# Graph layer on one core: the low halves of the scaled features move from DVE (one operation) to POOL (two operations)

## What is computed

```python
def _L0_gnn_ref(x, edge_index, W1, b1, W2, b2):
    ...
    deg = segment_sum(ones, dst); dinv = where(deg > 0, rsqrt(deg), 0.0)
    norm = dinv[src] * dinv[dst]
    ...
    h = x @ W;  msg = h[src] * norm[:, None];  agg = segment_sum(msg, dst)
    ...
xn = _layernorm(x, axis=-1)
x = x + _L0_gnn_ref(xn, ...) + _L0_mix_ref(xn[None], ...)[0]
x = x + _L0_ffn_ref(_layernorm(x, axis=-1)[None], ...)[0]
```

## Time and profile before

| | us |
|---|---|
| median of 2 runs (2003.83 and 2005.24) | 2004.53 |
| the profiled execution, its own time | 2000.85 |
| its span | 1999.0 |
| PE busy (94% of the span) | 1879.2 |
| DVE busy (59%) | 1182.2 |
| ACT busy (43%) | 851.9 |
| POOL busy (15%) | 299.6 |

### The profile page before, as it was taken

The page is one execution under the profiler, slowest core; times in us unless marked ns, Lnnn a source line. Parts: engine busy times, 40 slices in busy tenths (PEclk is TensorE's granted clock), DMA queues, the critical chain, the costliest instruction groups (busy, mean ns, idle before and its releaser), DMA issues. The chain is left out here.

```text
span 1999.0 us, 45233 instructions
## 1 busy us (share of the span) xinstructions
PE 1879.2 (94%) x18843; PEld 1409.5 (71%) x18843; DVE 1182.2 (59%) x2699; ACT 851.9 (43%) x1970; POOL 299.6 (15%) x417
## 2 busy tenths in 40 slices
PE   3599989999999999999979999999999999999598
PEld 3255555555555555555569999999999999998477
DVE  6899987666666666666515555555555555555322
ACT  1577765566566656666512222222222222222100
POOL 3143110000000000000020111111111111111033
PEclk7699989999999999999989999999999999999799
DMA  3133322323222232222344444444444444442087
GB/s 98 56 114 108 96 82 98 130 98 126 102 106 122 98 130 98 117 111 98 130 160 140 145 146 146 146 145 146 145 146 145 142 143 144 145 138 81 13 273 242
DMA packets 92701, 252.13 MB, mean 126 GB/s; under 512 B 14142, under 2 KB 59346, under 8 KB 79938
## 3 DMA queue, kind: packets, MB, share of 16 engines
q1 hardware_dynamic: 69225, 218.83, 30.8%
q10 hardware_dynamic: 21096, 25.65, 3.6%
q0 software_dynamic: 2176, 4.75, 0.9%
HBM read 131.99 MB, written 118.02 MB: 125 GB/s over the span
## 5 line engine op out<-in xcount | busy, mean ns | idle before, releaser
L1390 PE MATMUL ps<-hs,at 128*128 128x512 f16 x2401 | 667.1, 378 | 0.4 <-POOL at L1207 0.3
L1609 PE MATMUL ps<-at,big 128*128 128x128 f16 x9604 | 577.3, 219 | 6.5 <-DMA at<-at_scratch 6.5
L1609 PEld LDWEIGHTS ps<-at,big 128*128 128x128 f16 x9604 | 556.3, 98 | 34.3 <-issue 8.1
L1446 ACT CAST at<-ps 128x392 f16<-128x392 f32 x784 | 375.7, 487 | 286.7 <-PE ps L1351 271.3
L1351 PE MATMUL ps<-big 128*128 128x98 f16 x3136 | 470.8, 208 | 7.3 <-DVE big L1291 7.1
L1351 PEld LDWEIGHTS ps<-big 128*128 128x128 f16 x3136 | 297.0, 97 | 141.0 <-DVE big L1291 8.9
L1390 PEld LDWEIGHTS ps<-hs,at 128*128 128x128 f16 x2401 | 229.6, 97 | 148.2 <-issue 0.5
L1291 DVE TENSOR_TENSOR big<-iota_lo,key_lo 128x1024 f16<-128x1024 f16 x392 | 268.7, 685 | 0.0
L1291 DVE TENSOR_TENSOR big<-iota_hi,key_hi 128x784 f16<-128x784 f16 x392 | 219.3, 559 | 0.0
L1723 DVE SCALAR_TENSOR_TENSOR big<-ps,small,blogb 128x512 f32<-128x512 f32 x49 | 36.8, 751 | 230.6 <-PE ps L1645 230.6
L1826 POOL TENSOR_TENSOR key_lo<-key_lo,big 128x512 f32<-128x512 f32 (+1 forms) x49 | 61.9, 1264 | 706.6 <-ACT big L1784 706.6
(11 more groups left out here) (280 smaller groups left out, 2285.3 us busy)
## 6 DMA issues: line engine op xcount, KB each, us to landing
at_scratch<-at SPq DMA_DIRECT2D x49, 1568.0 KB, 5.2
at<-at_scratch SPq DMA_DIRECT2D x49, 1568.0 KB, 6.9
xT_scratch<-big SPq DMA_DIRECT2D x98, 128.0 KB, 1.8
big<-xT_scratch SPq DMA_DIRECT2D x49, 256.0 KB, 3.2
wT_scratch<-big ACTq DMA_DIRECT2D x49, 256.0 KB, 2.0
hs<-wT_scratch SPq DMA_DIRECT2D x49, 256.0 KB, 3.5
big<-in_x_dram SPq DMA_DIRECT2D x96, 128.0 KB, 2.3
x_scratch<-big ACTq DMA_DIRECT2D x48, 128.0 KB, 1.7
```

The lines of the kernel that those rows point to most:

```text
L1390: mm = te.matmul(ps[:, 2 + b, :], lhsT=at[:, b, k * P:(k + 1) * P], rhs=hs[:, k, :], start=(k == 0), stop=(k == T - 1))
L1446: a.copy(to.rearrange("p k (i j) -> p k i j", j=WIN), ps[:, BANKS[m % len(BANKS)], 0:UW * KC].rearrange("p (i k j) -> p k i j", i=UW, j=WI ...
L1609: mm = te.matmul(ps[:, b, c * NT:(c + 1) * NT], lhsT=hs2[:, k, h * C + c * P:h * C + (c + 1) * P], rhs=at[:, b, k * P:(k + 1) * P], start= ...
```

## The change

`halves` goes from DVE's stream. POOL gets `low_halves(t)`, between the gather and the addition of tile t: a product `xn * dsc` into a new buffer `scaled` (float32, 128 x 256), and the difference of `scaled` and the high half, written to `hs` as float16. Both count a semaphore `lows_made`, which also takes the place of `k4_zeroed`. `scaled` is one buffer, so the product of a tile waits for the difference of the tile before. `norm` gets a wait: the ring place of `xn` is written again only when the low half of the tile four before is done (`lows_made` counts the clearing of `k4_sum`, then two for each tile).

```diff
+            scaled = take([P, C])
...
                     if reached(t, RING):
                         dve.wait_ge(kx_done, t - RING + 1)
+                        dve.wait_ge(lows_made, 2 * (t - RING) + 3)
...
-                def halves(t, b):
-                    dve.wait_ge(hi_ready, t + 1)
-                    v.scalar_tensor_tensor(out=hs[0:rows(t), bass.ds(t, 1), C:2 * C].rearrange("p o c -> p (o c)"),
-                                           in0=xn[0:rows(t), b, 0:C], scalar=dsc[0:rows(t), bass.ds(t, 1)],
-                                           in1=hs[0:rows(t), bass.ds(t, 1), 0:C].rearrange("p o c -> p (o c)"),
-                                           op0=ALU.mult, op1=ALU.subtract)
...
-                    if reached(t, -1) and within(t, T - 1):
-                        halves(t + 1, (b + 1) % RING)
...
+                def low_halves(t, b):
+                    pool.wait_ge(hi_ready, t + 1)
+                    pool.wait_ge(lows_made, 2 * t + 1)
+                    g.tensor_scalar(scaled[0:rows(t), :], xn[0:rows(t), b, 0:C], dsc[0:rows(t), bass.ds(t, 1)], None,
+                                    ALU.mult).then_inc(lows_made, 1)
+                    pool.wait_ge(lows_made, 2 * t + 2)
+                    g.tensor_tensor(hs[0:rows(t), bass.ds(t, 1), C:2 * C].rearrange("p o c -> p (o c)"), scaled[0:rows(t), :],
+                                    hs[0:rows(t), bass.ds(t, 1), 0:C].rearrange("p o c -> p (o c)"),
+                                    ALU.subtract).then_inc(lows_made, 1)
...
                         gather_sources(t // WPS, t % WPS)
+                    low_halves(t, b)
                     pool.wait_ge(k4_ready, 2 * t + 2)
```

More of the change, by code:

```diff
@@ L623, in gps_layer @@
             k4_ready, k2n_ready, kx_done = sem("k4_ready"), sem("k2n_ready"), sem("kx_done")
-            k4_zeroed, k4_added = sem("k4_zeroed"), sem("k4_added")
+            lows_made, k4_added = sem("lows_made"), sem("k4_added")
             q2f_ready, q2_turned, q2T_stored = sem("q2f_ready"), sem("q2_turned"), sem("q2T_stored")
@@ L824, in _ @@
                 g = nc.gpsimd
-                g.memset(k4_sum, 0.0).then_inc(k4_zeroed, 1)
-                pool.wait_ge(k4_zeroed, 1)
+                g.memset(k4_sum, 0.0).then_inc(lows_made, 1)
+                pool.wait_ge(lows_made, 1)
                 def gather_sources(g, j):
```

## The result

The changed kernel takes 2019.24 us (median of 2 runs, 2018.86 and 2019.63) against 2004.53: ratio 1.0077, 95% interval 1.0057 to 1.0096. It is slower by 14.7 us; the forecast was 2006.0, the range ended at 2014. The profiled execution took 2019.63, its span is 2017.6.

What follows compares the result with a forecast made beforehand. PE was taken as the bound, except in seven key tiles, where it waits for DVE's normalised rows. L707 removed -2.7, holds +3.3, addition at L699 +0.9 sum to +1.5 on 2004.53: 2006.0 us, range 2000 to 2014.

Steps and rivals of the forecast that it cites:

- The step that failed: PE loses 2.08 us in each of seven key tiles (those with DVE's burst), nothing elsewhere but in first and last tiles.
- L707 removed, -2.7: Removing DVE's low halves shortens the path to L699 by 0.39 us in seven key tiles; nothing in 42 other tiles.
- Durations on POOL: POOL's new operations: product taken as 0.50 us, between 0.28 and 0.73; difference 0.67 us.
- Holds in the burst, +0.47 a key tile: Product and difference hold DVE's burst for 0.30 to 0.67 us a key tile; 0.47 taken, seven times +3.3 us.
- The walk through the tile: Key tile on the earlier timelines: product keeps L678 out +0.07 us, difference keeps L682 out +0.23.
- The addition at L699, +0.13: POOL's later addition holds L699 0 to 0.27 us more in key tiles; 0.13 taken, seven times +0.9 us.
- The gather: On POOL ahead of the product: 0.93 us in POOL's tile, with no hold on DVE in the sum.
- The new wait: norm's wait for the low half of four tiles earlier costs nothing while POOL keeps up.
- PE outside the key tiles: PE stays busy without a gap there, one tile taking 3.54 and 3.73 us.
- fall clear of the burst: Rival: product and difference meet DVE operations that POOL doesn't stretch; -2.7 us, or -4.2 with L699 missed; chance 0.20.
- set the pace of the stage: Rival: POOL becomes the bound, past a product of 0.65 us in early tiles; 2013.7 at product 1.0; chance 0.12.
- lengthen PE's ordinary tiles: Rival: DVE is held in every tile, 42 other tiles costing up to 0.42 us each, up to 2022; chance 0.10.

Runs made afterwards that it cites:

- e2: Changed kernel with four extra unused PE products one tile ahead of PE's wait in each of the seven key tiles: 2009.05 us, ratio 1.0019.
- e7: Kernel before, with the burst's last operation made twice, the first time into a spare tile, nothing new on POOL: 2018.98 us, ratio 1.0077.
- e10: Kernel before with the low halves made by nobody, zeros set once by POOL ahead of the first tile: 2009.72 us, ratio 1.0032.
- e6: Changed kernel with POOL's product also waiting for k2n of its tile: 2010.92 us, ratio 1.0037.
- e4: Changed kernel with xn in a ring of eight in place of four: 2017.55 us, ratio 1.0054.
- e5: Both makers: DVE's low halves as before, POOL's product and difference into a spare tile: 2031.44 us, ratio 1.0143.
- e11: Changed kernel with the burst's five operations laid over four tiles: 2003.68 us, ratio 0.9996.
- e3: Changed kernel with POOL's product waiting, in the seven key tiles, for the xn behind the burst: 2006.67 us, ratio 1.0004.

## Why the prediction was wrong, point by point

*The step that failed* is the one that turns DVE's lateness into time. It stands at the start, where a key tile loses 2.08 us "and nothing elsewhere but in its first and last tiles", and the sum takes it over: each hold counts at its own length, seven times, so a longer wait of PE costs its own length and no more. The sum had no term for the clock behind the wait, though the earlier trace rows has the clock as a column, at 1.00, and no step of mine asked whether it would stay there. e2 puts it back at 1.00 and takes 12.1 us out of the stage; e7 brings it down without the change. At the full clock the kernel would have come out at some +4 in the stage, by the growth of PE's waits. In e2, which also pays for its four products, it is +6.0, and e2's median, 2009.05 beside 2005.75, is inside the range.

*L707 removed, -2.7.* The right path and the wrong size: 1.6 by e10, because the burst moves onto the end of the gather, and where there is no gather L699 is held longer.

*Durations on POOL.* The difference was right (0.67 taken, 0.70 as a mean). The product was taken as 0.50, near the one-input row; with nothing in its way it takes 0.95 (at 132.35 us), above the bound of 0.73. The Trainium skill (GPSIMD Engine Reference, section 4.1, Engine selection) has one-input work at roughly line rate; measured, it was slower here than the addition with two inputs. The guess from L296, another operation at another size, was no bound.

*Holds in the burst, +0.47 a key tile.* Measured 0.19 + 0.07 + 0.35 = 0.61 in five key tiles, 0.65 in the last two, inside 0.30 to 0.67. The walk through the tile had the 0.07 of the third operation right and put 0.23 on the fifth; it had nothing on the first. *The addition at L699, +0.13:* 0.62 before and 0.62 after. *The gather* was priced at nothing, since L721 beside it was as short as ever in the kernel before. It costs 0.42 once POOL's next operation stands ready behind it (e6). So four of the seven key tiles came out at +0.64 at the full clock, not at +0.21; the first grew more, the last two less.

*The new wait* costs nothing, as said (e4). *PE outside the key tiles:* ahead of the first burst, and behind two of the key tiles, 3.54 and 3.73 as said; behind the other five not.

*The rivals.* POOL did not fall clear of the burst. It did not set the pace of the stage either, though the sign that I set for that, a product over 0.7, came. The sum put 0.14 between any two POOL instructions, which makes 2.89 + 0.95 = 3.84 of a tile ahead of the burst; measured it is 3.57, with gaps of 0.04 and 0.08 around the product. But this rival was nearer than the 0.12 says: 3.57 is over PE's 3.54, and in e5 and e11 POOL has next to no idle time. DVE's holds did not lengthen PE's ordinary tiles, 3.54 and 3.73 at the full clock; how much of DVE's 0.57 at the first burst comes from holds ahead of it is not shown. The rule of the Trainium skill (SBUF — State Buffer, section Who interferes with whom), that the other one is shut out for the whole instruction, gave about 2011. DVE's holds in the burst stayed inside my shorter bounds; POOL's product, though, was kept out for 1.95 - 0.95 = 1.0 us in the key tile shown.

*What stays open:* which waits bring the clock down. In the changed kernel one of 2.13 us did (at 140.74 us), one of 2.14 did not (180.28), one of 1.77 did (215.31); in e6 one of 1.62 did not; in e3 one of 1.51 with one of 0.58 close behind did, in the kernel before none of the seven of 1.21 to 1.51. The length of the wait alone doesn't tell it. Also open is why a gather holds L716 in the changed kernel and L673 in e10, and neither L721 before nor L716 in e6: e6 shows what undoes it for L716, not how it comes about.

## What to carry to other kernels

When PE is the engine that the kernel lives on, price a longer wait of PE twice: by its length, and by a tile at half the clock that may follow it; look at the granted clock in windows behind each wait, and ask how much longer than today's the wait would be. An operation that is moved to POOL takes a price with it if DVE's operations lie beside it, and it can make DVE pay for a neighbour on POOL that cost nothing before, here the gather. Undo and redo one half at a time: here the addition alone cost 28 us and the removal alone gave 1.6 (in the profiled stage), and neither says what the two give together.

## What the runs showed of the hardware that was not expected

- TensorE's clock fell to 1.2 GHz in the middle of a stage, behind many of the waits of 1.77 to 3.5 us, and behind some shorter ones with another close behind (e3: 1.11 and 0.77, 1.51 and 0.58); the tile behind then took up to 6.75 us (e4) in place of 3.73.
- A gather on POOL made a 128 x 256 operation of DVE take 0.77 in place of 0.35 when POOL's next operation was runnable, from the same offset of 0.31 us. Another gather made L673 0.17 longer with POOL's next operation not runnable (e10).
- Very small operations of DVE are held too: L712, on 128 x 2, took 0.69 in place of 0.16 beside POOL's addition (e3).
- POOL's product of a tensor with a per-partition number took 0.95 us for 128 x 256, its addition of two tensors 0.73.
